# Odd chunks' first weight block split by quarters inside the projections, side inputs added ahead of the loop, and a second attention one slot longer, in a two-layer cross-attention kernel

## The chip, the core and the metric

The kernel runs on one core of a Trainium2 chip. It has TensorE (PE in the rows; its weight loads are PEld), VectorE (DVE), ScalarE (ACT), GpSimd (POOL) and SyncE (SP, here the queue that issues DMAs). The metric is the device time of one execution in microseconds (us), the median of the runs shown. About 0.3% (11 us) is the smallest change that a measurement of this kernel can tell from none.

## What is computed

Two layers on x (4 batches, 1024 rows, 512 features) with a context of 64 rows per batch. Layer 0 is a cross attention of 16 heads with a bias tensor, fside, that is added twice to the scores. Layer 1 is a fake-quantised self attention over the 1024 rows, a fake-quantised cross attention on the same context, and a gated feed-forward.

```python
# layer 0
scores = (q @ wq + bq)(k @ wk + bk)^T / 8 + fside + fside
out    = softmax(scores) (v @ wv + bv) @ wo + bo + x
x      = layernorm(out) * ln_g + ln_b
# layer 1; fq(t, d, zp) = (clip(round(t / d) + zp, 0, 255) - zp) * d
x = attn(ln(x), ln(x)) + x          # self attention, 16 heads of 32
x = attn(ln(x), context) + x        # "second attention"
h = ln(x) @ ff_w1 + ff_b1           # 512 -> 4096, split into a and g
x = (a * gelu(g)) @ ff_w2 + ff_b2 + x
# attn: softmax(fq(q) fq(k)^T / sqrt(32)), quantised, times fq(v), @ wo + bo
```

Products of this precision are made of three matmuls each: an operand is split into a high and a low part (hi, lo), and hi x hi, hi x lo and lo x hi are summed.

## The kernel before

Each batch is two chunks of 512 rows, so there are eight chunks n = 0 to 7; even ones (0, 2, 4, 6) come first in a batch, odd ones second. A batch runs `cross(even)`, `cross(odd)`, then `self_attention(even)`, `middle(even)`, `self_attention(odd)`, `middle(odd)`. Every engine has its own copy of these functions and its own instruction queue in order; they meet at semaphores. The feed-forward of a chunk is not a stage of its own: it is cut into 48 steps of 12 matmuls, and `feed` (called by `host`) places them at numbered slots of later stages, by the plans FROM_S (for even chunks: 28 steps in the next self attention and 20 in the middle) and FROM_A (for odd chunks: 8 in each of the next two cross stages, 18 in the self attention, 14 in the middle). The order around the change is thus written out by hand: by the slots of the loops and by the plans.

**The cross stage.** In layer 0 the query and key weights are folded per batch into blocks M0 and M1 (the heads' halves), the value and output weights into N0 and N1. A block is 4 quarters k = 0 to 3 of 128 x 512. It is loaded as one fp32 tile `mixed`; ScalarE makes `w_hi` (`block_high`, L1152), GpSimd `w_lo` (`block_low`, L873, one instruction per quarter). PE transposes x (L1889, banks xT); ScalarE and VectorE split these into `ht_hi` (L1207) and `ht_lo` (L1349). Then a loop i = 0 to 10 follows: on PE the scores `s0` of step i (12 matmuls with M0, from i = 4 with M1, always into PSUM bank 0), the transposes `p0T` of step i - 2 (L1906), and the output product with N of step i - 3. VectorE takes s0 out of bank 0 with the side input `fbias` (L1502), takes the maximum (L1506) and subtracts it (L1509); ScalarE does the exp (L1219), VectorE the sum (L1515), GpSimd the scaling of e (L912). Before L1502 of a step, GpSimd has to have added `crow`, a row per batch, to that step's `fbias` (L905). GpSimd also adds the bias row `bo` to x once per chunk (`add_bias`, L885, 128 x 2048). So bank 0, and with it the next s0, waits for L1502, and this for L905.

Before: GpSimd's queue at an odd chunk's start is `block_low` of M0 and of N0 (8 instructions), `add_bias`, and then, from inside the loop, L905. For an even chunk N0's four quarters are at i = 0 and 1. ScalarE makes M0's and N0's high parts of an odd chunk after the 12 roundings of q1, k1 and v1 (`quantise`, L1090) of the even chunk ahead.

**The middle stage.** Slots 0 to 9 are o1, the norm and q2. Slots 10 to 17 are the second attention, s = 0 to 7, four tiles t: at s PE places the hosted step, s2(s) (L2027), p2T(s - 2) (8 transposes of w2b, L2035, all into bank 0), a2(s - 3) (L2044) and o2(s - 4) (12 matmuls). VectorE at s: the hosted step's work (L1476 or L1439), maximum (L1618) and subtraction (L1621) of s, sum (L1625 to L1629) of s - 1, `w2T` (L1634) of s - 2, which also frees bank 0, then the low part of a2 and the residual with the variance. GpSimd scales e (L998) and makes w2b (L1003). Slots 18 to 21 are the tail with the transposes h3T.

## Time and profile before

| what | value |
|---|---|
| median of 3 runs | 3563.54 us |
| lowest and highest | 3556.68 and 3568.96 us |
| profiled execution | 3564.55 us, span 3562.7 us |
| mean granted TensorE clock | 0.909 of full speed |
| busy: TensorE, VectorE, ScalarE, GpSimd | 84%, 62%, 47%, 42% of the span |

The span goes from the first to the last instruction of the profiled execution; 1.9 us of its time lie outside. The first 180 us are a set-up, then each batch takes about 811 us; the last 120 us are the last chunk's feed-forward alone. A row of the timeline gives start, duration, engine, line, operation and shape, and in brackets how long the engine sat idle just before and who released it. Idle time of an engine off the chain costs nothing. TensorE's clock is granted at one of two levels, 1.2 or 2.4 GHz, and a window's mean is given as a share of the higher.

### The profile page before, as it was taken

The page shows a single profiled execution, that of the slowest core. Times are in us where ns is not written, and L with a number is a line of the kernel's source. Part 1 is how long each engine was busy: PE and PEld are TensorE (multiplying, and loading weights), DVE is VectorE, ACT ScalarE, POOL GpSimd, SP SyncE. Part 2 cuts the span into 40 slices and gives each one's busy share as a digit, 9 for nine tenths or more (in the row PEclk, how much of TensorE's full clock was granted, in tenths as well). Part 3 has the DMA queues.
Part 4 walks back from the last instruction along what each step waited for, and adds up shares of the span by engine and source line. Part 5 has one row for each costly group of instructions (what it writes and reads, how often), then busy time and mean ns, then how long its engine had stood idle before and what let it go on. Part 6 is the DMA issues. An engine that isn't in the chain of part 4 may idle for free.

```text
span 3562.7 us, 50726 instructions
## 1 busy us (share of the span) xinstructions
PE 2979.5 (84%) x19712; PEld 2166.1 (61%) x19712; DVE 2193.1 (62%) x3543; ACT 1670.1 (47%) x2678; POOL 1506.3 (42%) x1165
## 2 busy tenths in 40 slices
PE   5467677798788889899887989889887888898899
PEld 5345545456576756656666755656766655655777
DVE  2263596785464587587564587587464588588421
ACT  4223275584333275376333276376323267277221
POOL 2364254465454154354364254354363345254221
PEclk9688856799899989899999999999999999999999
DMA  6934302234452312323452322232443321331434
GB/s 189 325 143 136 121 4 101 78 113 178 146 180 83 142 66 96 134 86 127 138 181 92 137 74 96 97 122 84 165 155 115 136 81 66 119 131 72 154 142 165
DMA packets 200621, 442.68 MB, mean 124 GB/s; under 512 B 95040, under 2 KB 103488, under 8 KB 182464
## 3 DMA queue, kind: packets, MB, share of 16 engines
q1 hardware_dynamic: 187968, 437.83, 34.3%
q10 hardware_dynamic: 12416, 1.62, 0.3%
q8 instruction: 158, 2.59, 0.3%
q14 instruction: 79, 0.65, 0.1%
HBM read 369.67 MB, written 65.54 MB: 122 GB/s over the span
## 4 chain that ended last, share of the span: by engine, by line
PE 52%; DVE 22%; POOL 9%; ACT 8%; issue 5%; DMA 3%; SPq 1%; ACTq 1%; POOLq 0%; DVEq 0%
PE psum L1685 15%; PE psum L1686 14%; PE psum L1687 14%; DVE mx L1565 8%; DVE w1T L1584 4%; PE psum L1967 3%; POOL w_lo L873 3%; ACT e L1256 2%; PE psum L1955 2%; DVE den L1571 2%; POOL x L885 1%; ACT psum L1146 1%; PE psum L1981 1%; DMA fw_lo<-pieces 1%; ACT ht_hi L1145 1%
## 5 line engine op out<-in xcount | busy, mean ns | idle before, releaser
L940 POOL TENSOR_SCALAR w1b<-e,rec 128x1024 f16<-128x1024 f32 x512 | 574.7, 1122 | 731.8 <-DVE rec L1573 534.7
L1565 DVE TENSOR_REDUCE mx<-psum 128x1 f32<-128x1024 f32 x512 | 622.4, 1217 | 36.5 <-PE psum L1956 36.4
L1256 ACT ACTIVATE e<-psum,nb,scale 128x1024 f32<-128x1024 f32 x512 | 617.5, 1206 | 16.8
L1685 PE MATMUL psum<-h_hi,fw_hi 128*128 128x512 f32 x1024 | 465.3, 454 | 17.8 <-DVE h_lo L1349 9.0
L1686 PE MATMUL psum<-h_lo,fw_hi 128*128 128x512 f32 x1024 | 417.8, 408 | 0.0
L1687 PE MATMUL psum<-h_hi,fw_lo 128*128 128x512 f32 x1024 | 416.4, 407 | 0.0
L1584 DVE TENSOR_SCALAR w1T<-psum 128x1024 bf16<-128x1024 f16 x512 | 348.7, 681 | 94.3 <-PE psum L1967 89.4
L1967 PE MATMUL psum<-ident,w1b 128*128 128x128 f16 x4096 | 351.0, 235 | 64.7 <-DVE w1T L1584 61.8
L1967 PEld LDWEIGHTS psum<-ident,w1b 128*128 128x128 f16 x4096 | 260.1, 105 | 233.4 <-issue 197.8
L1685 PE MATMUL psum<-w_hi,ht_hi 128*128 128x512 f32 x640 | 266.8, 417 | 72.7 <-DVE e L1502 42.3
L1439 DVE TENSOR_TENSOR x<-psum,x 128x512 f32<-128x512 f32 x224 | 152.3, 685 | 260.3 <-PE psum L1687 259.9
L879 POOL TENSOR_TENSOR rstd<-ve,mhalf 128x1 f32<-128x1 f32 x128 | 86.9, 679 | 495.2 <-DVE ve L1447 495.1
L1685 PEld LDWEIGHTS psum<-h_hi,fw_hi 128*128 128x128 f32 x1024 | 200.4, 196 | 136.5 <-issue 99.1
L1250 ACT ACTIVATE nb<-mx,nscale 128x1 f32<-128x1 f32 x512 | 149.9, 293 | 248.5 <-DVE mx L1565 240.9
L1686 PE MATMUL psum<-w_lo,ht_hi 128*128 128x512 f32 x640 | 259.4, 405 | 0.0
L1687 PE MATMUL psum<-w_hi,ht_lo 128*128 128x512 f32 x640 | 257.9, 403 | 0.0
L959 POOL TENSOR_TENSOR u_lo<-gate,u_hi 128x512 fp32r<-128x512 f32 x128 | 164.5, 1287 | 208.7 <-ACT u_hi L1182 203.1
L1685 PE MATMUL psum<-fw_hi,u_hi 128*128 128x512 f32 x512 | 226.4, 442 | 26.9 <-POOL u_lo L959 10.4
L1687 PEld LDWEIGHTS psum<-h_hi,fw_lo 128*128 128x128 f32 x1024 | 202.0, 197 | 47.4
L1349 DVE TENSOR_TENSOR ht_lo<-psum,ht_hi 128x512 fp32r<-128x512 f32 x160 | 108.5, 689 | 186.3 <-ACT psum L1146 132.3
L873 POOL TENSOR_TENSOR w_lo<-mixed,w_hi 128x512 fp32r<-128x512 f32 x128 | 169.4, 1349 | 123.0 <-ACT w_hi L1152 123.0
L1956 PE MATMUL psum<-k_odd,q_turned 32*128 32x512 bf16 x512 | 219.0, 428 | 0.0
(180 smaller groups left out, 6125.1 us busy)
## 6 DMA issues: line engine op xcount, KB each, us to landing
fw_hi<-pieces SPq DMA_DIRECT2D x168, 512.0 KB, 3.3
fw_lo<-pieces SPq DMA_DIRECT2D x168, 512.0 KB, 4.3
w_hi<-kept SPq DMA_DIRECT2D x48, 1024.0 KB, 4.8
w_lo<-kept SPq DMA_DIRECT2D x48, 1024.0 KB, 7.9
mixed<-mixed SPq DMA_DIRECT2D x32, 1024.0 KB, 4.9
fbias<-in_fside_Bx16xSxS SPq DMA_DIRECT2D x64, 256.0 KB, 3.0
unsplit<-in_L_xattn_ff_w SPq DMA_DIRECT2D x24, 512.0 KB, 5.2
pieces<-fw_hi SPq DMA_DIRECT2D x24, 512.0 KB, 2.6
```

The lines of the kernel that those rows point to most:

```text
L873: pool.tensor_tensor(w_lo[s][:, k, :], w_mixed[s][:, k, :], w_hi[s][:, k, :].bitcast(F32), ALU.subtract).then_inc(block_lo_done.sem, 1)
L940: pool.tensor_scalar(w1b[u % NH][:], e1[u % NE][:], rec1[:, u % 8:u % 8 + 1], HALF, ALU.mult, ALU.add).then_inc(w1_ready.sem, 1)
L959: pool.tensor_tensor(u_lo[:, m, :], gate[:, m, :], u_hi[:, m, :].bitcast(F32), ALU.subtract).then_inc(u_lo_done.sem, 1)
L1256: act.activation(e1[s % NE][:], psum[:, i:i + 2, :].rearrange("p i n -> p (i n)"), ACT.Exp, bias=nb1[:, s % 4:s % 4 + 1], scale=scale[:, 0:1],
L1439: return emptied_bank(dve.tensor_tensor(xt, bank(bank_of(key)), xt, ALU.add), key)
L1565: dve.tensor_reduce(mx1[:, s % 4:s % 4 + 1], psum[:, i:i + 2, :].rearrange("p i n -> p (i n)"), AX, ALU.max).then_inc(maxed1.sem, 1)
L1584: emptied_bank(dve.tensor_scalar(w1T[u % 8][:].rearrange("p k q -> p (k q)"), bank(bank_of(key)).bitcast(FP16), -HALF, W_HIGH, ALU.add, AL ...
L1685: pe.matmul(o, s_hi, m_hi, start=first, stop=False)
L1686: pe.matmul(o, s_hi, m_lo, start=False, stop=False)
L1687: return pe.matmul(o, s_lo, m_hi, start=False, stop=last)
L1956: ins = pe.matmul(bank(i + 1), q1_turned[turned, hg, t * P:t * P + P], k1[1][turned, hg, :], start=True, stop=True)
L1967: ins = pe.transpose(bank(bank_of(key)).bitcast(FP16)[:, k * P:k * P + P], w1b[u % NH][:, k * P:k * P + P], ident16[:])
```

## The change

The changes are of four kinds.

1. **M0 of odd chunks by quarters.** ScalarE makes quarter m of the next odd chunk's M0 right behind the rounding of v1's tile m. PE waits for the low part quarter by quarter, not for the last. N0 of odd chunks is made where the even chunks have it: on ScalarE behind `ht_hi`, on GpSimd at i = 0 and 1.
2. **Side inputs sooner.** GpSimd adds crow to the first three fbias tiles ahead of the loop: at odd chunks behind M0's low part, at even chunks (from n = 2) in the middle stage ahead, between M0's low part and the bias row ff_b2. Those of later steps are added at the end of slot i for step i + 1. SyncE issues the odd chunk's first three fbias loads before the odd chunk's blocks.
3. **x's bias in halves.** `bo` is added to x in two instructions of 128 x 1024, at i = 4 and i = 7.
4. **Second attention one slot longer.** p2T moves from s - 2 to s - 3, a2 from s - 3 to s - 4, o2 from s - 4 to s - 5 on PE, and the work that answers them on the other engines; the sum and w2b stay. M_SLOTS is 23. FROM_A's middle slots 16, 18, 20 become 17, 19, 21; FROM_S leaves out 16, 21 and 22.

```diff
-M_SLOTS = 22
+M_SLOTS = 23
-FROM_S = host_quarters(0, 28, [s for s in range(M_SLOTS) if s not in (16, 21)])
-FROM_A = host_quarters(8, 18, (0, 1, 2, 3, 4, 6, 10, 11, 12, 13, 15, 16, 18, 20))
+FROM_S = host_quarters(0, 28, [s for s in range(M_SLOTS) if s not in (16, 21, 22)])
+FROM_A = host_quarters(8, 18, (0, 1, 2, 3, 4, 6, 10, 11, 12, 13, 15, 17, 19, 21))
...
 # SyncE, cross
-                if n == 0 or c > 0:
+                if n == 0:
                     for i in range(3):
                         load_fbias(n, i)
...
                 if c == 0:
+                    for i in range(3):
+                        load_fbias(n + 1, i)
                     load_block((n + 1, "M0"))
...
 # GpSimd
             def block_low(key, ks):
                 s = SLOT[key]
-                pool.wait_ge(block_hi_done.sem, block_hi_done.at(key))
                 for k in ks:
+                    pool.wait_ge(block_hi_done.sem, block_hi_done.at((*key, k)))
...
+            def add_bias_half(n, bias, half):
+                xc = x[:, n % 3 * NT + 2 * half:n % 3 * NT + 2 * half + 2, :]
+                row = rows[bias][:].rearrange("p (o d) -> p o d", o=1).broadcast_to((P, 2, D))
+                ins = pool.tensor_tensor(xc, xc, row, ALU.add)
+                if half == 1:
+                    ins.then_inc(bias_added.sem, 1)
...
+            def add_crow(n, i):
+                number = n * STEPS0 + i
+                half = i // NT
+                pool.wait_ge(fbias_loaded[number % 3], 16 * (number // 3 + 1))
+                f = fbias[number % 3][:].rearrange("p h s -> p (h s)")
+                pool.tensor_tensor(f, f, crow[:, 512 * half:512 * half + 512], ALU.add).then_inc(fbias_ready.sem, 1)
...
-                wait_filled(pool, ("xT", n, KT - 1))
-                add_bias(n, "L0_xattn_bo")
-                pool.wait_ge(batch_loaded.sem, batch_loaded.at(n // NC))
+                if n == 0:
+                    pool.wait_ge(batch_loaded.sem, batch_loaded.at(0))
+                    for i in range(3):
+                        add_crow(0, i)
...
                 # in the loop, behind the scaling of e(i - 2)
-                    if i < 2 and n % NC == 0:
+                    if i < 2:
                         block_low((n, "N0"), range(2 * i, 2 * i + 2))
...
+                    if i == 4:
+                        wait_filled(pool, ("xT", n, KT - 1))
+                        add_bias_half(n, "L0_xattn_bo", 0)
...
+                    if i == 7:
+                        add_bias_half(n, "L0_xattn_bo", 1)
+                    if 3 <= i + 1 < STEPS0:
+                        add_crow(n, i + 1)
...
                     block_low((n + 1, "M0"), range(4))
-                    block_low((n + 1, "N0"), range(4))
+                    for i in range(3):
+                        add_crow(n + 1, i)
...
 # ScalarE, cross
                     for m in range(4):
                         quantise((kind, n, m), inv[:, i:i + 1])
+                        if kind == "v1" and n % NC < NC - 1:
+                            block_high((n + 1, "M0"), m, m)
...
-                if n % NC < NC - 1:
-                    block_high((n + 1, "M0"))
-                    block_high((n + 1, "N0"))
...
 # TensorE, cross
-                        if t == 0:
-                            pe.wait_ge(block_lo_done.sem, block_lo_done.at((n, f"M{half}", 3)))
                         wait_empty(key)
-                        done(token_major(bank(0), (n, f"M{half}"), t, of_ht_hi, of_ht_lo, wait=when_split("xT", n, i == 0)), key)
+                        done(token_major(bank(0), (n, f"M{half}"), t, of_ht_hi, of_ht_lo, wait=when_mixed(n, half, t)), key)
...
 # TensorE, middle (the same shift on the other engines)
-                    t = s - 2
+                    t = s - 3
                     if 0 <= t < NT:
                         key = ("p2T", n, t)
```

GpSimd's queue at the start of an odd chunk's cross stage (n = 5), in the kernel before; L873 is w_lo (M0 and N0), L885 the bias bo, L905 the adding of crow, L912 the scaling of e:

```order
512 L873 TENSOR_TENSOR w_lo<-mixed,w_hi 128x512 x8
513 L885 TENSOR_TENSOR x<-x,row_L_xattn_bo 128x2048
514 L905 TENSOR_TENSOR fbias<-fbias,crow 128x512 x3
515 L912 TENSOR_TENSOR e_0<-e_0,row_scale 128x512
516 L873 TENSOR_TENSOR w_lo<-mixed,w_hi 128x512 x2
517 L905 TENSOR_TENSOR fbias<-fbias,crow 128x512
```

And in the changed kernel, where these lines are L875, L893 (a half), L903 and L925:

```order
508 L875 TENSOR_TENSOR w_lo<-mixed,w_hi 128x512 x4
509 L903 TENSOR_TENSOR fbias<-fbias,crow 128x512 x3
510 L875 TENSOR_TENSOR w_lo<-mixed,w_hi 128x512 x4
511 L925 TENSOR_TENSOR e_0<-e_0,row_scale 128x512
512 L875 TENSOR_TENSOR w_lo<-mixed,w_hi 128x512 x2
513 L903 TENSOR_TENSOR fbias<-fbias,crow 128x512
514 L925 TENSOR_TENSOR e_1<-e_1,row_scale 128x512
515 L875 TENSOR_TENSOR w_lo<-mixed,w_hi 128x512 x2
516 L903 TENSOR_TENSOR fbias<-fbias,crow 128x512
517 L925 TENSOR_TENSOR e_2<-e_2,row_scale 128x512
518 L893 TENSOR_TENSOR x<-x,row_L_xattn_bo 128x1024
```

The bias is no longer between w_lo and fbias, and N0's four quarters now follow the first three fbias.

VectorE in an odd chunk's second attention (n = 3), from the maximum of tile 2 on, before; L1634 is w2T, the answer to p2T:

```order
1590 L1618 TENSOR_REDUCE row_max<-psum 128x16
1591 L1621 TENSOR_TENSOR e_2<-psum,row_max 128x1024
1592 L1625 TENSOR_REDUCE row_sum<-e_1 128x16
1593 L1627 TENSOR_SCALAR row_sum<-row_sum,delta 128x16
1594 L1629 RECIPROCAL row_scale<-row_sum 128x16
1595 L1634 TENSOR_SCALAR w2T<-psum 128x1024
1596 L1476 SCALAR_TENSOR_TENSOR gate<-psum,col_L_xattn_ff_b,gate 128x512
1597 L1618 TENSOR_REDUCE row_max<-psum 128x16
```

After (w2T is L1658, the hosted gate L1500, the maximum L1642):

```order
1590 L1642 TENSOR_REDUCE row_max<-psum 128x16
1591 L1645 TENSOR_TENSOR e_2<-psum,row_max 128x1024
1592 L1649 TENSOR_REDUCE row_sum<-e_1 128x16
1593 L1651 TENSOR_SCALAR row_sum<-row_sum,delta 128x16
1594 L1653 RECIPROCAL row_scale<-row_sum 128x16
1595 L1500 SCALAR_TENSOR_TENSOR gate<-psum,col_L_xattn_ff_b,gate 128x512
1596 L1642 TENSOR_REDUCE row_max<-psum 128x16
1597 L1645 TENSOR_TENSOR e_3<-psum,row_max 128x1024
1598 L1649 TENSOR_REDUCE row_sum<-e_2 128x16
1599 L1651 TENSOR_SCALAR row_sum<-row_sum,delta 128x16
1600 L1653 RECIPROCAL row_scale<-row_sum 128x16
1601 L1658 TENSOR_SCALAR w2T<-psum 128x1024
```

The first w2T now stands behind the maximum, subtraction and sum of the following tiles.

TensorE in an even chunk's second attention (n = 4), where the plan FROM_A hosts nothing in slot 14, before (four rows around p2T(0), L2035; L2027 is s2, L1685 the hosted step):

```order
7560 L1687 MATMUL psum<-h_hi,fw_lo 128x512
7561 L2027 MATMUL psum<-k,q2T 128x256 x4
7562 L2035 MATMUL psum<-ident,w2b 128x128 x8
7563 L1685 MATMUL psum<-h_hi,fw_hi 128x512
7564 L1686 MATMUL psum<-h_lo,fw_hi 128x512
```

After (L2058 is s2, L2066 p2T, L2075 a2, L1709 to L1711 the hosted step):

```order
6631 L1711 MATMUL psum<-h_hi,fw_lo 128x512
6632 L2058 MATMUL psum<-k,q2T 128x256 x4
6633 L2066 MATMUL psum<-ident,w2b 128x128 x16
6634 L2075 MATMUL psum<-w2T,v 64x128 x8
6635 L1709 MATMUL psum<-fw_hi,u_hi 128x512
6636 L1710 MATMUL psum<-fw_lo,u_hi 128x512
```

p2T(0) and p2T(1) stand side by side, with no hosted step between them.

## Rows read from the trace of the kernel before

**Rows 1.** The page: shares of the chain that ended last, by line
```profile
PE psum L1685 15%; PE psum L1686 14%; PE psum L1687 14%; DVE mx L1565 8%; DVE w1T L1584 4%; PE psum L1967 3%; POOL w_lo L873 3%; ACT e L1256 2%; PE psum L1955 2%; DVE den L1571 2%; POOL x L885 1%; ACT psum L1146 1%; PE psum L1981 1%; DMA fw_lo<-pieces 1%; ACT ht_hi L1145 1%
```

**Rows 2.** Timeline, TensorE, cross stage of odd chunk 5: start, us, what, [idle before]
```profile
1927.48 0.50 PE L1685 MATMUL psum<-w_hi,ht_hi 128*128 128x512 f32 x1 [2.60 <-POOL w_lo L873]
...
1938.82 0.79 PE L1685 MATMUL psum<-w_hi,ht_hi 128*128 128x512 f32 x1 [8.32 <-DVE e L1502]
...
1944.97 0.50 PE L1685 MATMUL psum<-w_hi,ht_hi 128*128 128x512 f32 x1 [0.86 <-DVE e L1502]
...
1953.67 0.66 PE L1906 MATMUL psum<-ident,e 128*128 128x128 f32 x4 [1.79 <-POOL e L912]
```

**Rows 3.** Timeline, GpSimd, the same stretch
```profile
1922.42 9.95 POOL L873 TENSOR_TENSOR w_lo<-mixed,w_hi 128x512 fp32r<-128x512 f32 x8 [29.97 <-ACT w_hi L1152]
1932.33 4.49 POOL L885 TENSOR_TENSOR x<-x,row_L_xattn_bo 128x2048 f32<-128x2048 f32 x1
1936.78 3.72 POOL L905 TENSOR_TENSOR fbias<-fbias,crow 128x512 f32<-128x512 f32 x3
```

**Rows 4.** Timeline, ScalarE, the same stretch
```profile
1919.77 0.78 ACT L1090 ACTIVATE qt<-psum,rounder,inv 128x512 f32<-128x512 f32 x1 [1.94 <-PE psum L1687]
1920.45 3.70 ACT L1152 ACTIVATE w_hi<-mixed 128x2048 fp32r<-128x2048 f32 x2
1924.05 2.04 ACT L1207 ACTIVATE ht_hi<-psum 128x512 fp32r<-128x512 f32 x4
```

**Rows 5.** Timeline, VectorE, the same stretch
```profile
1924.67 2.48 DVE L1349 TENSOR_TENSOR ht_lo<-psum,ht_hi 128x512 fp32r<-128x512 f32 x4 [3.33 <-ACT ht_hi L1207]
```

**Rows 6.** Timeline, TensorE (two rows) and GpSimd (one), even chunk 4
```profile
1814.82 0.66 PE L1906 MATMUL psum<-ident,e 128*128 128x128 f32 x4 [1.42 <-POOL e L912]
...
1820.01 0.66 PE L1906 MATMUL psum<-ident,e 128*128 128x128 f32 x4 [1.76 <-POOL e L912]
...
1812.02 1.75 POOL L905 TENSOR_TENSOR fbias<-fbias,crow 128x512 f32<-128x512 f32 x1
```

**Rows 7.** Timeline, TensorE, cross stages of chunks 0 and 1
```profile
185.42 0.80 PE L1685 MATMUL psum<-w_hi,ht_hi 128*128 128x512 f32 x1 [10.58 <-POOL w_lo L873]
...
205.74 0.65 PE L1906 MATMUL psum<-ident,e 128*128 128x128 f32 x4 [1.76 <-POOL e L912]
...
315.42 0.80 PE L1685 MATMUL psum<-w_hi,ht_hi 128*128 128x512 f32 x1 [9.76 <-POOL w_lo L873]
...
341.82 0.66 PE L1906 MATMUL psum<-ident,e 128*128 128x128 f32 x4 [1.78 <-POOL e L912]
```

**Rows 8.** Timeline, TensorE, second attention of odd chunk 3, even chunk 4
```profile
1746.24 1.03 PE L2035 MATMUL psum<-ident,w2b 128*128 128x128 f16 x8 [4.16 <-POOL w2b L1003]
...
1759.12 0.77 PE L2035 MATMUL psum<-ident,w2b 128*128 128x128 f16 x8 [3.83 <-POOL w2b L1003]
...
1776.16 0.47 PE L1685 MATMUL psum<-fw_hi,u_hi 128*128 128x512 f32 x1 [1.84 <-POOL u_lo L959]
...
2268.39 1.03 PE L2035 MATMUL psum<-ident,w2b 128*128 128x128 f16 x8 [4.05 <-POOL w2b L1003]
...
2281.30 1.03 PE L2035 MATMUL psum<-ident,w2b 128*128 128x128 f16 x8 [6.82 <-POOL w2b L1003]
```

**Rows 9.** Timeline, VectorE, the same two stages
```profile
1747.39 0.63 DVE L1634 TENSOR_SCALAR w2T<-psum 128x1024 bf16<-128x1024 f16 x1
...
1751.55 1.22 DVE L1618 TENSOR_REDUCE row_max<-psum 128x16 f32<-128x1024 f32 x1 [2.88 <-PE psum L2027]
...
1755.63 0.63 DVE L1634 TENSOR_SCALAR w2T<-psum 128x1024 bf16<-128x1024 f16 x1
...
2269.93 0.63 DVE L1634 TENSOR_SCALAR w2T<-psum 128x1024 bf16<-128x1024 f16 x1
```

**Rows 10.** Busy times by window: PE, PEld, DVE, ACT, POOL, granted clock, DMA
```profile
1938.00:1944.00 6.00, 5.18 (x12) 3.80 (x12) 2.90 (x3) 2.92 (x3) 2.50 (x3) 0.52 0.19 44
```

**Rows 11.** One line's instructions, L1509: durations in ns, least, median, most
```profile
L1509 DVE TENSOR_TENSOR e<-e,row_max x64: 691/907/1573, 192.6 to 2792.5; 128x512 f32<-128x512 f32 x64
```

63 lines of the change are left out of this document (34 added, 29 removed).

## The prediction, made before the changed kernel was run

> **What bounds the kernel now.** I first read the page's busy shares and the chain that ended last. TensorE is busy 84% of the span and holds the three largest shares of the chain; the chain leaves it for short pieces on VectorE and GpSimd, among them w_lo (L873, 3%) and the bias row (L885, 1%) [rows 1]. So no engine is full: the time is TensorE's work plus the gaps in which it waits. I then listed TensorE's gaps over 0.9 us with their releasers, stage by stage. In the stages that the change touches there are two families.
>
> The first is the start of the cross loop. In odd chunk 5 TensorE waits 2.60 us for GpSimd's w_lo of M0, does s0(0), and waits 8.32 us for VectorE's L1502 to free bank 0 [rows 2]. L1502 itself waits for fbias. GpSimd's rows show why: from 1922.42 it makes eight quarters of w_lo (9.95 us, 1.24 each), then the bias (4.49), then three fbias (3.72, 1.24 each) [rows 3]. It could not start sooner, since ScalarE makes both high parts in 3.70 us behind the last rounding at 1919.77, and ht_hi only behind those [rows 4].
>
> The second is the second attention: p2T(0) waits 4.16 us and p2T(2) 3.83 us in odd chunk 3, 4.05 and 6.82 us in even chunk 4, always for GpSimd's w2b [rows 8].
>
> A gap costs more than itself: in 1938 to 1944, right behind the 8.32 us, TensorE is granted 0.52 of full speed, thus mostly the 1.2 GHz level [rows 10].
>
> **Part A, odd cross stages.** For chunk 5, at the old times: M0's quarters are made in the pauses of ScalarE between roundings (the last waited 1.94 us for TensorE [rows 4]), so behind the last only one quarter is left, about 0.6 us, a quarter of half of 3.70 plus the fixed cost. It ends at 1921.1 instead of 1924.05; ht_hi (2.04) ends at 1923.1, and ht_lo, which follows it half a microsecond later (2.48 for four, ended 1927.15) [rows 4, 5], at 1924.3. GpSimd has M0's low part at 1921.1 + 1.24 = 1922.3, and fbias(0), (1), (2) at 1923.6, 1924.8 and 1926.1. TensorE's hosted step ran until 1927.48 - 2.60 = 1924.9, so s0(0) starts there with no wait. It takes about 2.8 us (1938.82 - 8.32 - 1927.48 = 3.0 with its end). L1502 is then ready at once, and the wait between s0(0) and s0(1) is what a clean one costs, 0.86 [rows 2]: s0(1) starts at 1928.5 instead of 1938.82 and at full clock, s0(2) at 1932.2. N0's quarters keep GpSimd until 1931.1, before e(0) is ready for it (about 1934.9), so p0T(0) is at 1936.0 and p0T(1), with its old spacing of about 5 us (1.79 of it idle), at 1940.8. Before it was at 1953.67: 12.9 us, of which I count 12.8 per odd chunk from 3 on. For chunk 1 GpSimd must first do a preparation for another weight, and M0 ends at 315.4 as before. There s0(0) is fed by quarters and ends at about 316.7, fbias(0) is ready by then, and N0's quarters hold GpSimd until 324.2; p0T(1) comes at about 330.3 instead of 341.82 [rows 7]: 11.5. Sum 3 x 12.8 + 11.5 = **49.9 us**. Nothing behind it is late: the odd chunk's N0 and M1 land before they are used, and the later waits in the stage (1.1 to 2 us each, for z, ht_lo and the pieces of the feed-forward) move along, since their loads are issued behind work of the same stage. Bounds: 36 (TensorE gets only the 8.32 and 6.7 us waits back to 1.1) and 60 (no gaps at all up to p0T(1)).
>
> **Part B, even cross stages.** The bias of bo leaves the front, and e(0) no longer stands behind the third fbias, which ended just before it (1812.02 + 1.75) [rows 6]. By the same chain as above p0T(0) comes at 1813.0 instead of 1814.82: 1.8 us for each of chunks 2, 4 and 6. Chunk 0 has GpSimd's 4.5 us of bias in the open: s0(0) is fed by quarters and ends at 186.1; fbias(0) at 186.7; N0 ends on GpSimd at 194.2; p0T(1) at about 200.2 instead of 205.74 [rows 7], 5.5 us. Sum **10.9 us**, bounds 0 and 15.
>
> **Part C, odd second attentions.** p2T(0) now has one more hosted step and s2(3) ahead of it, about 3.2 us of work under its 4.16 us wait. But p2T(t + 1) writes bank 0, which w2T(t) frees, and w2T now stands behind the next tiles' maximum, subtraction and sum. From the first row of that block to w2T VectorE needs 1755.63 - 1751.55 = 4.08 us [rows 9]. VectorE had been idle 2.88 us there, for s2(3) [rows 9]; that idle time goes, and VectorE becomes the bound: at 1747.39 it does the gate (0.66), then the block (4.08) and w2T (0.62), and p2T(1) starts at 1752.8. Then a2(0) and the hosted step of slot 15 run without a wait, and p2T(2) starts at 1756.7 instead of 1759.12 [rows 8]: 2.4 us, and a hosted step (2.8) that came after it is already done. The wait of 1.84 us for u_lo shrinks to about 1.1. Two or three stretches at half clock, 1.5 us each, become one or two. Sum 2.4 + 2.8 + 0.7 + 1.3 = 7 per chunk, x 4 = **28 us**. Bounds 2 x 4 = 8 (VectorE's queue gives back all but the idle 2.88) and 11 x 4 = 44 (both waits gone with their half clock).
>
> **Part D, even second attentions.** Here slot 14 hosts nothing, and p2T(0) and p2T(1) stand side by side. p2T(1) waits for w2T(0): 2269.93 + 0.66 + 4.08 + 0.62 = 2275.3 [rows 9], about 6 us of idle TensorE. The hosted step behind it needs u_lo, which stands behind w2b(2), 2.6 us more by VectorE's and GpSimd's queues (nearest row 1.84 [rows 8]). p2T(2) is then at about 2282.3, later than the old 2281.30 [rows 8], with one hosted step (2.8) more done. I take 1 us of gain each for chunks 2, 4, 6 and 1.3 for chunk 0, which hosts nothing: **4.3 us**, bounds -12 and +16.
>
> **Part E, GpSimd work that moves beside VectorE.** The work's amount hardly changes. L1509 takes 691 ns alone and up to 1573 beside GpSimd [rows 11]. The bias halves (half of 4.49, 2.2 us) now lie beside it in mid-loop. TensorE's pace there is about 6 us per step and VectorE's work under 5, so I take 0; uncovered it is up to 1.5 us for each of 16 halves, 24 us.
>
> The Trainium skill, GPSIMD Engine Reference, Key points, says that GpSimd shares its SBUF interfaces with VectorE, in contention with instructions that have two SBUF inputs. L1509 is such a one, and the spread from 691 to 1573 ns agrees [rows 11]; L1349, with one operand in PSUM, ran four times in 2.48 us beside w_lo [rows 3, 5]. It speaks against putting the bias into the loop; its price is the bound just given.
>
> **The sum.** 49.9 + 10.9 + 28 + 4.3 = 93 us. From the profiled 3564.55 that leaves 3471.5; the median is 1.0 lower, so **3471 us**.
>
> **The rivals.** (1) *The second attention gives nothing*: VectorE's longer way to w2T, and the missing hosted step in even chunks, cost as much as the waits they replace. For it: the 4.08 us in front of w2T are new on p2T's path. Against: 2.88 us of VectorE's idle time goes. C and D are 0 to 8: 3564 - 61 + 0 = 3503, with some of C about 3495. (2) *Contention in the loop*: the moved GpSimd work stretches VectorE's L1509 at each half, and the later order of fbias (behind e's scaling) makes L1502 late again. 93 - 24 = 69: 3495; by the page's rule that is what every half beside L1509 would give if VectorE were short of time. (3) *Slower*: GpSimd's new order closes a loop, since fbias(i + 1) now stands behind e(i - 2), which waits for VectorE's sum, and L1502 of i + 1 frees the bank that PE needs. With 4.8 us of GpSimd work in a slot of about 6 it holds; if a slot took 2.5 us longer, five slots in eight chunks cost 100 us, and the kernel would be at 3564 - 93 + 100 = 3571. It decides the sign from 2.3 us a slot. (4) *The quarters do not help*, because ht_lo sets the start: then only the 2.60 us stay, 4 x 2.6 = 10: 3481. It lies in the range.
>
> **Chances.** Forecast (with 4) 0.68, rival 1 0.15, rival 2 0.10, rival 3 0.04, and 0.03 for no change in sum. Faster by over 0.3%, 0.93; within, 0.04; slower, 0.03. The range is 3448 to 3510: the low end is A at 55 and C at 44, the high end reaches rival 1 and part of rival 2.
>
> **What would show it.** In the profile after: no wait for w_lo and one of about 1 us for L1502 at the start of an odd cross loop (A); in chunk 0 the bias gone from the front of GpSimd's queue (B); p2T(1) released by w2T and no longer p2T(0) by w2b (C, D), with about 6 us before p2T(1) in even chunks. A is wrong if TensorE waits over 3 us for fbias or p0T there; C if the time from the first s2 to the next stage's x transposes shrinks by under 4 us; E if L1509's median grows well over 907 ns and TensorE waits for L1502 in mid-loop.

## The result and the profile after

The changed kernel takes 3479.16 us (median; 3474.16 to 3479.6) against 3564.76 (3556.68 to 3568.96) before, a ratio of 0.9759 with a 95% interval of 0.974 to 0.9779. The profiled execution took 3479.19 us, its span is 3477.3, so the span shrank by 85.4 us; 3471 had been predicted, with 3448 to 3510 as the range.

The shares of the chain that ended last, from the page of after: by engine, and the first of the line shares.

```profile
PE 53%; DVE 24%; ACT 8%; issue 5%; POOL 5%; DMA 3%; SPq 1%; ACTq 1%; POOLq 0%; DVEq 0%
```

GpSimd's w_lo (L875 now) has 1% of it where it had 3 [rows 1], and the bias row is no longer among the first. The new code is longer, so line numbers move by 2 to 24: w_lo L873 is L875 now, L885 is L887, e L912 is L925, u_lo L959 is L980, w2b L1003 is L1024, ht_lo L1349 is L1373, gate L1476 is L1500, L1502 is L1526, L1509 is L1533, the sum L1627 is L1651, w2T L1634 is L1658, the three-part products L1685 to 1687 are L1709 to 1711.

To see where the time went I cut both spans at the first transposes of x, the first p0T, the first s1 and the first s2 of each chunk (TensorE's timeline) and added the stages up, in us. The first s1 ends the odd cross stage, the first s2 starts the second attention, and its row holds the tail behind it too:

| stage (chunks) | before | after | gain | predicted |
|---|---|---|---|---|
| cross, odd (A) | 551.3 | 506.3 | 45.0 | 49.9 |
| of it, x's transposes to p0T(0) | 119.2 | 72.4 | 46.8 | |
| cross, even (B) | 507.2 | 499.8 | 7.4 | 10.9 |
| second attention, odd, and what follows the last (C) | 382.9 | 357.6 | 25.3 | 28 |
| second attention, even (D) | 199.4 | 192.6 | 6.8 | 4.3 |
| self-attention and slots 0 to 9 of the middle, all | 1750.8 | 1750.3 | 0.5 | 0 |

Of these 85 us, 68.5 are TensorE's idle time and 16.6 its busy time, which is longer where its clock is at the lower level.

**The odd cross stage** of chunk 5: TensorE's timeline. A row has the start in us, the duration, engine, line, operation, tiles, and the idle time before it with its releaser; these are the starts of s0(1), s0(2), p0T(0) and p0T(1), its only waits over 0.3 us from s0(0) on.

```profile
1885.41 0.50 PE L1709 MATMUL psum<-w_hi,ht_hi 128*128 128x512 f32 x1 [0.86 <-DVE e L1526]
1889.33 0.50 PE L1709 MATMUL psum<-w_hi,ht_hi 128*128 128x512 f32 x1 [0.86 <-DVE e L1526]
1892.83 0.66 PE L1937 MATMUL psum<-ident,e 128*128 128x128 f32 x4 [0.45 <-POOL e L925]
...
1898.06 0.66 PE L1937 MATMUL psum<-ident,e 128*128 128x128 f32 x4 [1.79 <-POOL e L925]
```

The waits of 2.60 and 8.32 us [rows 2] are gone: s0(0) has none in front of it, and s0(1) 0.86. ScalarE's and GpSimd's timelines of the same stretch show how:

```profile
1874.67 0.62 ACT L1177 ACTIVATE w_hi<-mixed 128x512 fp32r<-128x512 f32 x1
1876.71 0.78 ACT L1114 ACTIVATE qt<-psum,rounder,inv 128x512 f32<-128x512 f32 x1 [1.42 <-PE psum L1711]
1877.39 0.62 ACT L1177 ACTIVATE w_hi<-mixed 128x512 fp32r<-128x512 f32 x1
1877.91 2.05 ACT L1233 ACTIVATE ht_hi<-psum 128x512 fp32r<-128x512 f32 x4
```
```profile
1878.09 1.34 POOL L875 TENSOR_TENSOR w_lo<-mixed,w_hi 128x512 fp32r<-128x512 f32 x1 [1.39 <-ACT w_hi L1177]
1879.38 3.79 POOL L903 TENSOR_TENSOR fbias<-fbias,crow 128x512 f32<-128x512 f32 x3
1883.13 5.47 POOL L875 TENSOR_TENSOR w_lo<-mixed,w_hi 128x512 fp32r<-128x512 f32 x4
1891.73 1.04 POOL L925 TENSOR_TENSOR e<-e,row_scale 128x512 f32<-128x512 f32 x1 [3.13 <-DVE row_scale L1541]
```

A quarter of w_hi costs 0.62 us (0.6 was predicted) and lies in ScalarE's pauses; one quarter of w_lo is left behind the last rounding; GpSimd ends N0 3.13 us before it gets e(0). In [rows 3] eight quarters and the bias, 14.4 us, stood between the last rounding and fbias; here it is one quarter, 1.34 us. Three quarters of M0 are made before that, N0's four and the bias later.

**The second attention**: TensorE's timeline, odd chunk 3 (p2T(1), the hosted step behind u_lo, the next hosted step that waits) and even chunk 4 (a hosted step, p2T(1), the step that needs u_lo).

```profile
1717.73 0.61 PE L2066 MATMUL psum<-ident,w2b 128*128 128x128 f16 x8 [2.00 <-DVE w2T L1658]
1731.75 0.47 PE L1709 MATMUL psum<-fw_hi,u_hi 128*128 128x512 f32 x1 [0.99 <-POOL u_lo L980]
1748.37 0.50 PE L1709 MATMUL psum<-fw_hi,u_hi 128*128 128x512 f32 x1 [1.73 <-DVE x L1463]
...
2212.63 0.50 PE L1709 MATMUL psum<-h_hi,fw_hi 128*128 128x512 f32 x1 [1.31 <-DVE gate L1500]
2222.68 1.01 PE L2066 MATMUL psum<-ident,w2b 128*128 128x128 f16 x8 [6.14 <-DVE w2T L1658]
2226.83 0.76 PE L1709 MATMUL psum<-fw_hi,u_hi 128*128 128x512 f32 x1 [2.56 <-POOL u_lo L980]
```

Neither p2T(0) nor p2T(2), which waited for w2b [rows 8], waits any more. VectorE's w2T is what p2T(1) waits for, and in even chunks for 6.14 us where "about 6" was predicted, with the 2.56 us for u_lo behind it (2.6 predicted).

### The profile page after: what moved, and what is told of

It is laid out like the page before. It is cut to its first block, busy times and chain, and to the rows that moved or that the text cites. A ratio compares the mean times of both kernels' runs of the same rounds, so it can differ in the third digit from the quotient of the medians.

```text
span 3477.3 us, 50794 instructions
## 1 busy us (share of the span) xinstructions
PE 2963.1 (85%) x19712; PEld 2152.9 (62%) x19712; DVE 2204.1 (63%) x3543; ACT 1671.5 (48%) x2690; POOL 1511.2 (43%) x1173
## 4 chain that ended last, share of the span: by engine, by line
PE 53%; DVE 24%; ACT 8%; issue 5%; POOL 5%; DMA 3%; SPq 1%; ACTq 1%; POOLq 0%; DVEq 0%
PE psum L1709 16%; PE psum L1710 14%; PE psum L1711 14%; DVE mx L1589 8%; DVE w1T L1608 4%; PE psum L1998 3%; ACT e L1280 2%; PE psum L1986 2%; DVE den L1595 2%; ACT psum L1170 1%; POOL w_lo L875 1%; DVE gate L1500 1%; DMA unsplit<-in_L_xattn_ff_w 1%; PE psum L2012 1%; DMA fw_lo<-pieces 1%
## 5 line engine op out<-in xcount | busy, mean ns | idle before, releaser
L1709 PE MATMUL psum<-h_hi,fw_hi 128*128 128x512 f32 x1024 | 463.1, 452 | 31.3 <-DVE h_lo L1373 10.0
L1711 PE MATMUL psum<-h_hi,fw_lo 128*128 128x512 f32 x1024 | 414.2, 404 | 0.0
L1709 PEld LDWEIGHTS psum<-h_hi,fw_hi 128*128 128x128 f32 x1024 | 198.9, 194 | 152.0 <-issue 98.2
L1709 PE MATMUL psum<-w_hi,ht_hi 128*128 128x512 f32 x640 | 259.2, 405 | 30.1 <-DVE e L1526 13.7
L1709 PE MATMUL psum<-fw_hi,u_hi 128*128 128x512 f32 x512 | 229.3, 448 | 30.0 <-POOL u_lo L980 13.7
L1711 PE MATMUL psum<-w_hi,ht_lo 128*128 128x512 f32 x640 | 252.7, 395 | 0.0
L980 POOL TENSOR_TENSOR u_lo<-gate,u_hi 128x512 fp32r<-128x512 f32 x128 | 164.3, 1285 | 202.9 <-ACT u_hi L1208 197.0
L1711 PEld LDWEIGHTS psum<-h_hi,fw_lo 128*128 128x128 f32 x1024 | 200.8, 196 | 47.0
L875 POOL TENSOR_TENSOR w_lo<-mixed,w_hi 128x512 fp32r<-128x512 f32 x128 | 175.5, 1395 | 113.9 <-ACT w_hi L1177 113.9
L1114 ACT ACTIVATE qt<-psum,rounder,inv 128x512 f32<-128x512 f32 x128 | 99.8, 780 | 248.4 <-PE psum L1711 248.4
```

What stands on the lines that cost most here:

```text
L875: pool.tensor_tensor(w_lo[s][:, k, :], w_mixed[s][:, k, :], w_hi[s][:, k, :].bitcast(F32), ALU.subtract).then_inc(block_lo_done.sem, 1)
L980: pool.tensor_tensor(u_lo[:, m, :], gate[:, m, :], u_hi[:, m, :].bitcast(F32), ALU.subtract).then_inc(u_lo_done.sem, 1)
L1709: pe.matmul(o, s_hi, m_hi, start=first, stop=False)
L1711: return pe.matmul(o, s_lo, m_hi, start=False, stop=last)
```

## The experiments

All were run beside the kernel before, which took 3562.0 to 3564.0 us in each set of runs; the ratios are to that. A difference of 5 us or less between two medians here lies within intervals that overlap, so the small pieces are read from the stages of the one traced execution of each kernel. Diffs are against the changed kernel.

### Each half of the change alone

The cross part alone: the middle has its old 22 slots and its old order, all else is new.

```diff
-M_SLOTS = 23
+M_SLOTS = 22
...
-                    t = s - 3
+                    t = s - 2
                     if 0 <= t < NT:
                         key = ("p2T", n, t)
```

> The kernel before with the cross stage's parts alone (M0 by quarters, side inputs sooner, N0 in the loop, bias in halves); second attention as before. Theory 1, the parts add up: the changed kernel's gain in the cross stages was 45 us in the odd ones and 7 in the even ones, so 3564 - 52 = 3512 us. Rival, the two parts share a gain (a shorter second attention only moved waits that the cross stage would take anyway): below 3500 or above 3525. In chunks 4 and 6 the time from the x transposes to the first p0T shows whether the missing gain of even chunks comes from the half clock behind them: about 17.9 us where TensorE's clock is full there, 19.4 where it is at half.

Measured: 3503.72 us (3501.57 to 3508.0), ratio 0.9833 (0.9815 to 0.9851). The odd cross stages gain 48.4 us and the even ones 9.9; the second attentions are 1.5 us longer, the self-attention part 2.9 shorter. That is 8 us below the 3512 that I expected, and not the rival's "below 3500". In chunks 2, 4 and 6 p0T(0) comes 18.1 us after x's first transpose, against 19.4 in the full change and 19.5 before.

The middle part alone: the opposite, only the longer second attention (23 slots, p2T three slots behind s2) with its loads.

> The kernel before with the longer second attention alone. Theory 1: 25 us from the odd middles and 7 from the even ones, 3564 - 32 = 3532 us, with p2T(1) released by w2T as in the changed kernel (2.0 us of wait in odd chunks, 6.1 in even ones). Rival: under 10 us of gain, 3554 or more, if the gain seen there was made by the stage before.

Measured: 3525.08 us (3522.95 to 3530.06), ratio 0.9894 (0.9879 to 0.991). The second attentions gain 27.0 us in the odd chunks and 6.5 in the even ones, so the rival that they give nothing is out; I had expected 3532. The two gains, 60 and 38, add to 98, and together they gave 85. By stages the 13 us that are missing have three parts. The cross part alone has 2.5 us less in the even cross stages than the full change and 3.4 less in the odd ones, though the code there is the same. The self-attention part, where nothing was changed, is 1747.9 and 1747.5 us in the two halves against 1750.8 before and 1750.3 in the full change: 5.7 us. And the cross stages of the middle alone, also unchanged, are 2.0 us shorter than before. The second attentions add up to within 0.1 us. For the first part the traces show the reason: TensorE's idle time in the cross stages is 150.7 us in the full change and 153.3 in the cross part alone, but its mean granted clock is 0.94 against 0.96. The other two vary from execution to execution in idle time as well as in clock and are not settled.

How such a stretch comes about can be seen in the even chunks. From x's first transpose to p0T(0) the full change and a later experiment (w2T first, below) wait at the same places for the same times in chunk 4. TensorE's rows, first of after, then of that kernel:

```profile
1754.67 0.66 PE L1922 MATMUL psum<-ident,x 128*128 128x128 f32 x4 [1.10 <-DVE h_lo L1373]
1756.01 0.79 PE L1922 MATMUL psum<-ident,x 128*128 128x128 f32 x4 [0.68 <-DVE h_lo L1373]
1764.58 0.50 PE L1709 MATMUL psum<-w_hi,ht_hi 128*128 128x512 f32 x1 [0.86 <-DVE e L1526]
```
```profile
1751.17 0.65 PE L1922 MATMUL psum<-ident,x 128*128 128x128 f32 x4 [1.10 <-DVE h_lo L1373]
1752.50 0.66 PE L1922 MATMUL psum<-ident,x 128*128 128x128 f32 x4 [0.68 <-DVE h_lo L1373]
1759.77 0.50 PE L1709 MATMUL psum<-w_hi,ht_hi 128*128 128x512 f32 x1 [0.86 <-DVE e L1526]
```

Yet from the second to the third row it is 8.57 us in one and 7.27 in the other. The windows (busy times of PE, PEld, DVE, ACT, POOL, then granted clock, DMA share, GB/s) of the same stretch, again after and then w2T first:

```profile
1756.00:1760.00 4.00, 4.00 (x13) 3.27 (x14) 2.75 (x5) 4.00 (x8) 3.56 (x1) 0.57 1.01 391
```
```profile
1753.00:1757.00 4.00, 4.00 (x19) 2.96 (x18) 3.25 (x6) 4.00 (x8) 3.07 (x1) 1.00 1.05 418
```

Thirteen matmuls against nineteen in 4 us, at a granted 0.57 (mostly the 1.2 GHz level) against 1.00 (2.4 GHz). The waits ahead of both are alike, and so are they in chunks 2, 4 and 6 of the execution of w2T first, which take 19.4, 18.1 and 18.1 us to p0T(0). So a stretch at half clock can come or not behind the same short waits, 1.3 us each time here.

### M's first block whole again

```diff
                        quantise((kind, n, m), inv[:, i:i + 1])
-                        if kind == "v1" and n % NC < NC - 1:
-                            block_high((n + 1, "M0"), m, m)
...
+                if n % NC < NC - 1:
+                    block_high((n + 1, "M0"))
```

> The changed kernel, but ScalarE makes M0's high part of the odd chunk in one instruction behind the last rounding. Theory 1, most of part A came from taking N0 and the bias out of the way of fbias: M0's low part ends 5 us later, but fbias only follows it, s0(1) starts 0.8 us and the first p0T about 1.2 us later, 4 x 1.2 = 5 us: 3484. Rival, the quarters carry the gain: 2.60 us of wait return at each odd chunk and fbias is late by 5, 4 x 5 to 8 = 20 to 30 us: 3500 to 3510.

Measured: 3483.61 us (3481.15 to 3487.89), ratio 0.9777 (0.9762 to 0.9792). To p0T(0) the odd chunks 3, 5 and 7 take 18.6 us instead of 16.3, chunk 1 takes 1.3 more: 8.3 us of the 46.8. The medians differ by 4.5 us, within overlapping intervals. I had expected 1.2 us in each chunk, so the total of 3484 came out by the wrong sum, but the rival's 20 to 30 us are out.

### The bias of bo back at the front of the loop

```diff
+                wait_filled(pool, ("xT", n, KT - 1))
+                add_bias(n, "L0_xattn_bo")
                 for i in range(STEPS0 + 2):
...
-                    if i == 4:
-                        wait_filled(pool, ("xT", n, KT - 1))
-                        add_bias_half(n, "L0_xattn_bo", 0)
...
-                    if i == 7:
-                        add_bias_half(n, "L0_xattn_bo", 1)
```

> The changed kernel with the bias of bo back, whole, at the front of GpSimd's cross loop, behind the fbias additions that now stand in the stage before. My theory of part A: what freed the start was that the eight quarters of low parts and the bias no longer stand ahead of fbias. Here only the bias (4.5 us) and N0's quarters (5.0) lie between the third fbias (chunk 5: 1926.1 by the prediction) and e(0), which is due at 1934.9: they end at 1935.6, so p0T(0) is 0.7 to 1.5 us later in each chunk, and in chunks 0 and 1, where GpSimd is late already, up to 4.5: about 3490. Rival: the bias at the front was the larger part of the gain by itself, 4.5 us in every chunk: 3515.

Measured: 3492.52 us (3489.5 to 3501.56), ratio 0.9809 (0.9794 to 0.9823), some 13 us more than after. Chunks 3, 5 and 7 take 18.1 us to p0T(0) instead of 16.3 (in chunk 5 TensorE now waits 2.31 us for e(0) at 1911.86), chunks 0 and 1 4.8 and 4.9 more. My expectation was 0.7 to 1.5 and up to 4.5: right in kind, a little low. It has no word on what chunks 2 and 4 did: 22.1 instead of 19.4 us. VectorE's and GpSimd's timelines, chunk 4:

```profile
1778.88 0.69 DVE L1527 TENSOR_REDUCE row_max<-e 128x8 f32<-128x512 f32 x1
1779.60 4.35 DVE L1530 TENSOR_TENSOR e<-e,row_max 128x512 f32<-128x512 f32 x1
1783.87 0.68 DVE L1523 SCALAR_TENSOR_TENSOR e<-fbias,psum 128x512 f32<-128x512 f32 x1
```
```profile
1769.29 4.57 POOL L887 TENSOR_TENSOR x<-x,row_L_xattn_ff_b 128x2048 f32<-128x2048 f32 x1
1773.82 4.63 POOL L887 TENSOR_TENSOR x<-x,row_L_xattn_bo 128x2048 f32<-128x2048 f32 x1
1778.40 5.01 POOL L875 TENSOR_TENSOR w_lo<-mixed,w_hi 128x512 fp32r<-128x512 f32 x4
```

The subtraction of the row's maximum (L1533 in after), 691 ns alone, took 4.35 us. It began at 1779.60, about when GpSimd began the second of its four w_lo (5.01 / 4 = 1.25 us apiece), and ended at 1783.95, 0.54 us behind the end of the fourth at 1783.41: it got in at none of the joints between them. In chunk 6 the same code took 1.85 us, from 2568.18 to 2570.04, and the w_lo that began with it ended at 2569.49, again 0.55 us earlier: there it got in at the next joint, and TensorE lost 0.2 us. The bias in front does not stand beside the subtraction; it moves w_lo onto it. This contention has a tail that the row of before, 1573 ns at most [rows 11], does not show.

### N0 split in the stage before again

The two places that make N0 in or ahead of the loop are then for even chunks alone.

```diff
+                if n % NC < NC - 1:
+                    block_high((n + 1, "N0"))
...
                     block_low((n + 1, "M0"), range(4))
+                    block_low((n + 1, "N0"), range(4))
                     for i in range(3):
                         add_crow(n + 1, i)
```

> The changed kernel with N0 of odd chunks split in the stage before again, as in the kernel before: its high part on ScalarE behind M0's quarters and ahead of ht_hi, its low part on GpSimd ahead of the three fbias. My theory: ht_hi comes 1.85 us later and fbias(0) some 5 us later (chunk 5: 1928 to 1929 instead of 1923.6), so s0(0) starts 1 to 2 us late and s0(1) waits 2 to 4 us for L1526: from the first x transposes to p0T(0) of odd chunks 3.5 us more, 19.8 instead of 16.3, x 4 = 14: 3493. Rival: there is slack for N0, and GpSimd is behind only by the bias: under 1.5 us per odd chunk, 3480 to 3485.

Measured: 3483.9 us (3481.63 to 3489.12), ratio 0.9782 (0.9769 to 0.9796). The stretch to p0T(0) is 1.5 us longer in chunks 3, 5 and 7 (17.8 against 16.3) and 6.0 in chunk 1: the rival's size for the three, more than mine for the one, and the total lies in the rival's 3480 to 3485. In chunk 5 TensorE's only longer wait is this:

```profile
1896.93 0.50 PE L1713 MATMUL psum<-w_hi,ht_hi 128*128 128x512 f32 x1 [2.37 <-DVE e L1530]
```

2.37 against 0.86 is the 1.5. Counted from x's first transpose, fbias(0) ends 5.5 us later than in after, about as I had it. But in after it ended 4.0 us before L1526 could use it (1880.68 against 1884.67), and I had not counted that slack.

### The bias whole in slot 4, and no bias

```diff
-                        add_bias_half(n, "L0_xattn_bo", 0)
+                        add_bias(n, "L0_xattn_bo")
...
-                    if i == 7:
-                        add_bias_half(n, "L0_xattn_bo", 1)
```

> The bias of bo is added to x whole, in slot 4 of the cross loop, instead of in halves in slots 4 and 7. My theory: GpSimd then has some 4.5 + 1.2 + 1.2 us of work in a slot of about 6 us, 1 us too much, and it is made up in the next slot, so 0 to 1 us per chunk: 3479 to 3487. Rival 3 of the prediction (GpSimd's order closes a loop, fbias behind e's scaling): the 2.2 us more in that slot all reach TensorE, in 8 chunks, 18 us: 3497.

Measured: 3484.08 us (3474.77 to 3492.95), ratio 0.9765 (0.9746 to 0.9785). The even cross stages take 124.8 to 125.0 us instead of 123.9 to 124.0, chunk 3's 124.8 instead of 124.0. TensorE's idle time is 1.3 to 1.6 us longer in each of these, and part of that is given back by a stretch at half clock less in this execution; the loop that rival 3 describes would give 2.2 in each of eight chunks and a total of 3497. The medians differ by 5 us, within intervals that overlap, so that the halves pay is a reading of the stages and not clear in the total.

```diff
                         wait_filled(pool, ("xT", n, KT - 1))
-                        add_bias_half(n, "L0_xattn_bo", 0)
+                        pool.sem_inc(bias_added.sem, 1)
...
-                    if i == 7:
-                        add_bias_half(n, "L0_xattn_bo", 1)
```

> The bias of bo is not added to x at all, so the result lacks it: the price of the two halves in the loop, with all their contention with VectorE. Part E of the prediction said 0: 3477 to 3480. Rival 2 (the halves stretch VectorE's operations with two SBUF inputs beside them, and TensorE feels it, up to 1.5 us for each of 16 halves): 3455 to 3470.

Measured: 3475.17 us (3464.25 to 3480.74), ratio 0.9741 (0.9722 to 0.9761), an interval that overlaps that of after (I had expected 3477 to 3480, rival 2 3455 to 3470). The result lacks the bias. The cross stages of chunks 2 to 5 take 123.9 or 124.0 us with the bias in the loop and 123.9 without, apart from chunk 5's 126.8 (below). One line's instructions, the subtraction of the maximum, in after and without the bias (ns: least, median, most):

```profile
L1533 DVE TENSOR_TENSOR e<-e,row_max x64: 691/1216/1819, 188.5 to 2715.3; 128x512 f32<-128x512 f32 x64
```
```profile
L1531 DVE TENSOR_TENSOR e<-e,row_max x64: 691/875/1853, 187.5 to 2704.1; 128x512 f32<-128x512 f32 x64
```

So the halves do slow VectorE, and TensorE feels none of it. The medians overstate by how much, since the 64 durations lie in two groups with a gap where the median falls: the mean is 1066 ns before, 1171 in after and 1015 without the bias.

### w2T ahead of the next tile's block

VectorE's five lines on w2T go from behind the next tile's sum to ahead of its maximum.

```diff
+                    t = s - 3
+                    if 0 <= t < NT:
+                        key = ("p2T", n, t)
+                        wait_filled(dve, key)
...
                     if s < NT:
                         key = ("s2", n, s)
```

> The changed kernel with one edit on VectorE: w2T of tile s - 3 stands ahead of the maximum, subtraction and sum of slot s. Theory 1, p2T(1) waits for w2T behind these 4.1 us: its wait of 2.0 us in odd chunks goes, that of 6.14 us in even ones falls to the one for w2b(1), about 3, and half-clock stretches go with it: 4 x 1.5 + 3 x 3 = 15 us, 3464. Rival, VectorE's total work is the bound and not its order: what p2T(1) gains, w2b(2) and (3) lose, 3475 to 3482.

Measured: 3473.54 us (3470.39 to 3476.05), ratio 0.9747 (0.9733 to 0.9762): 10 us short of what I expected, and a little below the rival. The second attentions of chunks 3 and 5 take 51.2 and 51.1 us against 53.1. But the order in after gave 53.1 or 53.2 in only half of the sixteen such stages of the eight runs that have it, and 51.5 or 51.6 in the others, with the same wait for w2T (2.00 and 2.01 us): in after the window behind that wait is

```profile
1716.00:1724.00 8.00, 6.27 (x45) 4.78 (x45) 6.65 (x12) 2.58 (x5) 6.98 (x6) 0.79 0.00 1
```

against 1.00 in the same window of the run with the whole bias. So 1.5 of the 2 us is a stretch at half clock, which the early w2T had in none of its eight, and 0.4 is the wait as such. In the even ones nothing is won (51.3 to 51.5 against 51.1 to 51.5): TensorE's timeline of chunk 4,

```profile
2214.82 0.70 PE L2066 MATMUL psum<-ident,w2b 128*128 128x128 f16 x8 [3.80 <-POOL w2b L1024]
2221.52 0.77 PE L1709 MATMUL psum<-fw_hi,u_hi 128*128 128x512 f32 x1 [5.43 <-POOL u_lo L980]
```

has 3.80 + 5.43 us of waits for GpSimd where after has 6.14 + 2.56. Counted from the first s2, p2T(1) starts 2.3 us sooner than in after and p2T(2) no sooner: the wait only moves from w2T to u_lo.

### Which slots host a step

The hosting slots of the even chunks' middle are changed. First slots 14 and 16 for 6 and 15:

```diff
-FROM_A = host_quarters(8, 18, (0, 1, 2, 3, 4, 6, 10, 11, 12, 13, 15, 17, 19, 21))
+FROM_A = host_quarters(8, 18, (0, 1, 2, 3, 4, 10, 11, 12, 13, 14, 16, 17, 19, 21))
```

> The changed kernel with the feed-forward quarters of the even chunks hosted in slots 13, 14 and 16 of the middle instead of 13 and 15 with 6: slot 14 now hosts a step, and slot 6 none. My theory: the 6.14 us in which TensorE waits for w2T between p2T(0) and p2T(1) of chunks 2, 4 and 6 are free for 2.8 us of hosted work, but the u_lo of that step stands behind w2b on GpSimd, so only 1 to 2.5 us of it are won: 3 x 1.7 = 5, thus about 3474, and the second attention of even chunks shrinks from 51.1 to about 49. Rival: the step moved out of slot 6 was itself cover there, and TensorE loses as much in the queries: 3479 to 3484, with the self-attention part longer by 1 to 2 us in even chunks.

Measured: 3470.23 us (3469.37 to 3473.36), ratio 0.9733 (0.9719 to 0.9746). The second attention of even chunks is 0.1 to 0.8 us shorter with one step more in it; the part before, with a step of 2.8 less, is 1.2 shorter in one chunk and no shorter in two, since the empty slot 6 bares this wait in chunk 4:

```profile
2184.67 0.47 PE L1709 MATMUL psum<-ht_hi,w_hi 128*128 128x512 f32 x1 [2.00 <-DVE ht_lo L1373]
```

Some 2 us come from this. Of the rest of what this execution has over after, 6.6 us lie in the odd cross stages, where nothing was changed. Chunk 7, TensorE's rows and the window behind them, of after:

```profile
2739.05 0.47 PE L1709 MATMUL psum<-fw_hi,u_hi 128*128 128x512 f32 x1 [2.96 <-issue]
2742.39 0.79 PE L1709 MATMUL psum<-fw_hi,u_hi 128*128 128x512 f32 x1 [0.76 <-DMA fw_lo<-pieces]
...
2740.00:2748.00 8.00, 7.24 (x23) 5.29 (x23) 0.69 (x1) 0.10 (x1) 0.00 (x0) 0.61 0.07 29
```

and of slot 14:

```profile
2731.59 0.47 PE L1709 MATMUL psum<-fw_hi,u_hi 128*128 128x512 f32 x1 [1.72 <-issue]
2734.45 0.50 PE L1709 MATMUL psum<-fw_hi,u_hi 128*128 128x512 f32 x1 [1.25 <-DMA fw_lo<-pieces]
...
2734.00:2742.00 8.00, 6.21 (x28) 4.82 (x28) 3.25 (x7) 0.00 (x0) 0.15 (x1) 1.00 0.00 0
```

The waits sum to 3.72 and 2.97; behind the longer pair the clock is 0.61 for 8 us, behind the other 1.00, and the stage is 127.4 us against 123.9. The length of the waits alone does not decide it: in before, 2.93 us of them at this place in chunk 3 were followed by such a stretch and 3.81 us in chunk 7 by none. And each kernel has one traced execution, so how often the stretch comes is not shown.

Both edits together:

> Both edits at once: VectorE reads w2T out of its bank before the next tile's block, and slot 14 hosts a step in even chunks instead of slot 6. If the bound in even chunks is GpSimd's w2b and the u_lo behind it, and slot 14 hides a part of it, the gains add: 3473.5 - 5 = about 3468. Rival: with w2T early the step in slot 14 only moves the wait for u_lo, and this gives what the early w2T gave alone, 3472 to 3475.

Measured: 3470.4 us (3469.88 to 3471.84), ratio 0.9732 (0.9719 to 0.9746). The stages add (157.7 odd as with w2T first, 190.5 even), the total is that of slot 14 alone: the cross tail took its 3 us in chunk 7 here. Between the rival and me, this decides nothing.

Then slot 14 for 15, with slot 6 kept and w2T first:

```diff
-FROM_A = host_quarters(8, 18, (0, 1, 2, 3, 4, 6, 10, 11, 12, 13, 15, 17, 19, 21))
+FROM_A = host_quarters(8, 18, (0, 1, 2, 3, 4, 6, 10, 11, 12, 13, 14, 17, 19, 21))
```

> VectorE reads w2T before the next tile's block, and in even chunks the step of slot 15 of the middle is hosted in slot 14 instead; slot 6 keeps its own. In the two slot experiments before this one, the step taken out of slot 6 cost 1.9 of the 2.8 us that it saved in its new place. My theory: the step in slot 14 lies in the wait for p2T(1), the one in slot 15 lay in front of a wait for w2b anyway, so this gains 1 to 2 us in each of chunks 2, 4 and 6 over the early w2T alone (3473.5): about 3469, and the second attention of even chunks 49 to 50 us. Rival: VectorE and GpSimd set the pace of all four tiles there (about 5 us each), whichever slot hosts: 51.3 as before, 3473.

Measured: 3479.55 us (3475.74 to 3482.05), ratio 0.9764 (0.9751 to 0.9778): a miss of 10 us, and not the rival either. Even second attentions take 54.5 to 54.7 us, 3.2 more than with w2T first alone. TensorE, chunk 4:

```profile
2224.57 0.77 PE L1709 MATMUL psum<-fw_hi,u_hi 128*128 128x512 f32 x1 [10.54 <-POOL u_lo L980]
```

Steps come in two kinds: those that make h's products need only a freed bank, those that take u need u_lo, which VectorE's gate and GpSimd's queue deliver a tile's block later. Taking slot 6 as a host made the eleventh step, of the second kind, fall in slot 14. Last, then, slots 14 and 16 for 12 and 15, slot 6 kept, w2T first, so that 13 and 14 both host the first kind:

```diff
-FROM_A = host_quarters(8, 18, (0, 1, 2, 3, 4, 6, 10, 11, 12, 13, 15, 17, 19, 21))
+FROM_A = host_quarters(8, 18, (0, 1, 2, 3, 4, 6, 10, 11, 13, 14, 16, 17, 19, 21))
```

> VectorE reads w2T before the next tile's block; in even chunks the feed-forward steps of slots 12 and 15 of the middle go to slots 14 and 16, and slot 6 keeps its own. From the three slot experiments: a step in slot 14 costs nothing if it is one that only needs the gate of the step before (it hid 2.8 us), and 10.5 us if it needs u_lo; a step missing in slot 6 bares a wait of 2.00 us for ht_lo. Here slot 13 and 14 both host steps of the first kind, the u_lo step comes in slot 16, and slot 6 is hosted. My theory: the second attention of even chunks takes 50.3 as with slot 14 and the early w2T, less up to 2.8 since slot 12's step is gone from it, and the part before it is 1.9 us shorter than there less the 2.8 of the step: together 1 to 2 us less than that kernel's for each of chunks 2, 4 and 6, about 3467. Rival: without a step in slot 12 TensorE only waits longer for VectorE's next block, nothing is won, 3470 to 3472.

Measured: 3468.12 us (3464.81 to 3472.68), ratio 0.973 (0.9713 to 0.9747). In the even second attention of chunk 4 two waits are left, 3.93 and 2.90 us, both for w2b:

```profile
2212.51 1.04 PE L2066 MATMUL psum<-ident,w2b 128*128 128x128 f16 x8 [3.93 <-POOL w2b L1024]
2222.15 1.03 PE L2066 MATMUL psum<-ident,w2b 128*128 128x128 f16 x8 [2.90 <-POOL w2b L1024]
```

The stage takes 50.0 to 50.2 us. This is the lowest median of the study, 11 us or 0.3% under the changed kernel. But the two intervals still overlap a little (0.9747 against 0.974), and this one and that of slot 14 alone do so almost wholly.

## Why the prediction was right, and where its terms were off

The total is 8 us above the forecast and 2 from rival 4's 3481, so by itself it does not tell the two apart; the rows do, below.

**A, 45.0 of 49.9.** The mechanism is as worked out for chunks 3, 5 and 7: s0(0) without a wait, 0.86 before s0(1), p0T(1) 1.79 behind. Chunk 1 still waits 6.66 us for w_lo in front of s0(0), where it was 9.76 [rows 7]. To p0T(0) the gain is 46.8, and undoing one piece at a time costs there 8.3 for M0 whole, 10.4 for the bias at the front and 10.5 for N0 in the stage before. That is 29 together; the other 18 us belong to no piece by itself, and no run undid two at once. Nor was the early adding of crow to fbias undone by itself: what it is worth is not shown. N0 and the bias each weigh more than the quarters that name the change, and none of the three is most of A. Of the 4.9 us that are missing, 3.1 are missing at p0T(0) already: chunk 1 gave 10.0 for 11.5, chunk 7 11.7 for 12.8. The other 1.8 are behind the stage's changed part. In chunks 5 and 7 the waits for feed-forward pieces (3.72 us in sum each, 2.89 in chunk 3) were followed by a stretch at half clock, some 3 us each (126.8 and 127.4 against 124.0 in chunk 3); in slot 14's execution they have none of it, and A is there 551.3 - 499.7 = 51.6. "The later waits move along" was right for the waits and silent on their clock.

**B, 7.4 of 10.9.** Chunk 0 gave 3.9 (131.9 to 128.0) of 5.5, chunks 2 and 4 only 0.2 and 0.3 of 1.8 each. The failed step is the 1.8 for p0T(0), which came 0.1 us sooner in each of chunks 2, 4 and 6: the waits in front of it did shrink in chunks 4 and 6, but the half clock behind x's transposes (at 1756 in chunk 4) took 1.3 us of it, and chunk 2 has that stretch in both kernels. With the cross part alone, where it runs at 1.00, p0T(0) comes 1.4 us sooner in each chunk, and B is 9.9. Chunk 6's stage gave 3.0 us at a place that the forecast does not name: in the kernel before, a wait for feed-forward pieces late in the stage, and a stretch at half clock behind it.

```profile
2680.33 0.47 PE L1685 MATMUL psum<-h_hi,fw_hi 128*128 128x512 f32 x1 [2.56 <-DMA fw_lo<-pieces]
...
2680.00:2688.00 8.00, 7.67 (x29) 6.23 (x30) 1.37 (x4) 2.42 (x2) 0.55 (x1) 0.79 0.23 91
```

In after that wait is 1.14 us, and the clock behind it stays at 1.00. The middle alone, with the old cross stage, has 2.51 us there, and every kernel with the new one 1.14 to 1.64; why is not shown. Without this place B is 4.4 of 10.9.

**C, 25.3 of 28.** Chunks 3, 5 and the last gave 7.4, 8.2 and 7.3 for 7 each (1.5 more where no half clock follows; the forecast's four terms add to 7.2). Chunk 1 gave 2.4, some 5 less. Half of that lies in the kernel before: there chunk 1 already took only 57.9 us against 60.5 in chunk 3, with nearly the same waits but a mean granted clock of 0.97 against 0.92. The other half lies in after, 55.5 against 53.1 us. There GpSimd also makes low parts of the first feed-forward weights, which I had not looked at; rows of VectorE, GpSimd and TensorE:

```profile
920.55 2.00 DVE L1651 TENSOR_SCALAR row_sum<-row_sum,delta 128x16 f32<-128x16 f32 x1
...
922.75 0.66 DVE L1500 SCALAR_TENSOR_TENSOR gate<-psum,col_L_xattn_ff_b,gate 128x512 f32<-128x512 f32 x1
```
```profile
920.17 4.66 POOL L968 TENSOR_TENSOR fw_lo<-unsplit,fw_hi 128x1024 fp32r<-128x1024 f32 x2
```
```profile
923.47 0.77 PE L1709 MATMUL psum<-h_hi,fw_hi 128*128 128x512 f32 x1 [2.47 <-DVE gate L1500]
```

An operation on 16 elements a row, 0.23 us at its least, takes 2.00 beside fw_lo: it ends at 922.55, just behind the first of the two fw_lo (4.66 / 2 = 2.33 us apiece, so at 922.50). The gate behind it is late, and TensorE waits 2.47 us for it where it waits 0.71 in chunk 3; its idle time in the stage is 9.1 us against 6.8. No run takes fw_lo away, so that this is the cause is read from the rows. The step that failed is "x 4", which took chunk 1 to be like the others.

**D, 6.8 of 4.3.** The waits are the forecast ones (6.14, 2.56). Chunk 4 gave 1.2 for 1; chunks 2 and 6 gave 2.6 and 2.4, and there the mean granted clock rose from 0.87 to 0.90, where chunk 4 has 0.90 in both kernels. So the excess is a stretch at half clock fewer in two chunks, which the forecast had not counted. Chunk 0 gave 0.7 for 1.3.

**E, 0 of 0.** TensorE has no wait over 0.3 us for L1526 in mid-loop, and without the bias the median is 4 us lower, not clear of noise, with equal stages. But the row that I took as the bound, 1573 ns, was no bound: after has 1819, and 4.35 us came up with the bias at the front, where the quarters of N0 ran in a row beside it. The operation next to it, which has one operand in PSUM, does not feel GpSimd at all, in ns:

```profile
L1526 DVE SCALAR_TENSOR_TENSOR e<-fbias,psum x64: 686/689/690, 187.1 to 2713.9; 128x512 f32<-128x512 f32 x64
```

The Trainium skill, SBUF — State Buffer, Who interferes with whom, says that VectorE and GpSimd share a pair of ports as an exclusive lock, held by the one that issues first for its whole instruction, where VectorE's has two SBUF inputs or runs in a 2-port mode. The 4.35 us go beyond it, since the operation passed three joints between GpSimd's instructions and got in behind the last alone. There the measurement decides. The 2.00 us above end as such a lock would, at the end of GpSimd's instruction; whether that operation, which has one SBUF input, ran in a 2-port mode no row tells.

**The rivals.** That the second attention gives nothing fell with the middle alone (33.5 us in its stages). Contention, at 24 us, fell with the run without the bias (4 us by the medians, within the noise), the closed loop with the whole bias in slot 4: about 1.4 us of idle time a chunk for 2.2 us more in a slot, and 3484 us where it needed 3497. Rival 4, that the quarters do not help and the 2.60 us stay, has almost the measured total, but no wait stands before s0(0) in any of chunks 3, 5 and 7, and M0 whole costs 8.3 us to p0T(0). The total came near it because B, A and C fell short for the reasons above.

## What to carry to other kernels

A chain that feeds the first step of a loop can be shortened as much by taking from it work that was merely issued ahead as by cutting its own pieces finer: here bias and N0 were worth 10 us each when undone alone, the finer M0 8. When a stage is stretched by a slot, ask for each queue what now stands ahead of the operation that frees the next bank, and which kind of hosted step falls into which slot: in slot 14 a step of one kind hid its 2.8 us of work in a wait, and one of the other kind waited 10.54 us and made the stage 3.2 us longer. And the price of contention has to be taken as a range from more than one phase; the worst row of one trace is not its bound.

## What the runs showed of the hardware

Two things that I had not expected. A VectorE operation, however small, can be held up until a GpSimd operation beside it ends: 2.00 us instead of 0.23 beside fw_lo, and on two elements a row up to 4129 ns (median 228), beside a bias of 4.55. Once one was held up through a whole run of them, 4.35 us instead of 0.69 beside w_lo.

```profile
L1595 DVE TENSOR_SCALAR den<-sum,delta x256: 218/228/4129, 432.0 to 3215.7; 128x2 f32<-128x2 f32 x128
...
2282.84 4.55 POOL L887 TENSOR_TENSOR x<-x,row_L_xattn_a_bo 128x2048 f32<-128x2048 f32 x1
...
2283.29 4.13 DVE L1595 TENSOR_SCALAR den<-sum,delta 128x2 f32<-128x2 f32 x1
```

And the granted clock differs behind waits that are equal to a hundredth, between executions and between chunks of one: 0.57 or 1.00 over 4 us behind 1.10 and 0.68 us of idle TensorE, 1.3 us each. At the feed-forward pieces it was 0.61 over 8 us behind waits of 3.72 us in sum and 1.00 behind 2.97, some 3 us each; but in before a stretch came behind 2.93 us and none behind 3.81. Such stretches are about 6 of the 13 us by which the two halves gave more apart than together, and a reason why kernels within 5 us of each other need more than one profile to be told apart.
